# First attention of a four-layer network: values stationary in 32-column tiles, scores in 64-row tile pairs, ScalarE copies ahead of exponentials, outputs turned in their own bank

## The reference, cut to what matters

```python
q = _qdq(x) @ _qdq(wq).T + bq
kv = cond @ wkv.T + bkv
...
attn = jax.nn.softmax(jnp.einsum('bnhd,bmhd->bhnm', q, k) * scale, axis=-1)
o = jnp.einsum('bhnm,bmhd->bnhd', attn, v).reshape(B, N, C)
out = _qdq(o) @ _qdq(wp).T + bp
```

## Time and profile before

| | us |
|---|---|
| three runs | 843.74, 844.09, 846.97 (median 844.09) |
| span of the profiled execution | 847.4 |
| PE busy in the span | 760.9 (90%) |
| DVE busy | 576.4 (68%) |
| ACT busy | 379.8 (45%) |
| POOL busy | 374.7 (44%) |

### The profile page before, as it was taken

How to read it: one execution, slowest core, us unless ns; L and a number is a source line. 1 busy time by engine, 2 the same in 40 slices (tenths; PEclk the granted TensorE clock), 3 DMA queues, 4 the chain that set the end, 5 groups by cost and what they waited for, 6 DMA issues and landing times.

```text
span 847.4 us, 13816 instructions
## 1 busy us (share of the span) xinstructions
PE 760.9 (90%) x4696; PEld 437.9 (52%) x4696; DVE 576.4 (68%) x1247; ACT 379.8 (45%) x652; POOL 374.7 (44%) x397
## 2 busy tenths in 40 slices
PE   7999999999999887777888989889999999999883
PEld 4557776544357322222333635445558967687531
DVE  5988876379664889998999896876521135025854
ACT  3444443311101798887999253655203343421211
POOL 3524304035132277787888542201160047971435
PEclk9999999999999999998999999999999999988998
DMA  9500002002520789999999300620953142991013
GB/s 299 115 1 1 1 1 78 17 0 48 102 50 1 125 160 188 176 185 176 193 186 185 53 1 24 153 89 14 223 147 122 44 143 70 291 218 46 5 15 36
DMA packets 225996, 84.36 MB, mean 100 GB/s; under 512 B 188003, under 2 KB 224000, under 8 KB 225936
## 3 DMA queue, kind: packets, MB, share of 16 engines
q1 hardware_dynamic: 222992, 78.33, 43.1%
q0 software_dynamic: 2944, 5.25, 2.7%
HBM read 33.21 MB, written 8.40 MB: 49 GB/s over the span
## 4 chain that ended last, share of the span: by engine, by line
PE 55%; DVE 13%; DMA 11%; issue 9%; POOL 7%; ACT 3%; SPq 1%; POOLq 0%; DVEq 0%; ACTq 0%
DMA hT<-hT 6%; PE psum L485 5%; POOL hT L1249 5%; PE psum L660 4%; DMA xn<-hT 4%; PE psum L1759 3%; PE psum L640 3%; DVE psum L1314 3%; PE psum L524 3%; PE psum L1430 2%; PE psum L489 2%; DVE cx L2387 2%; PE psum L2037 2%; PE psum L465 2%; PE psum L612 2%
## 5 line engine op out<-in xcount | busy, mean ns | idle before, releaser
L1314 DVE TENSOR_SCALAR_CACHE_REDUCE psum<-psum,arena 128x1024 f32<-128x1024 f32 x128 | 158.0, 1285 | 11.4 <-PE psum L1136 11.0
L336 POOL TENSOR_TENSOR rstd<-ve,neg_half 128x1 f32<-128x1 f32 x64 | 39.2, 616 | 181.2 <-DVE ve L326 180.4
L1136 PE MATMUL psum<-arena 128*128 128x512 bf16 x256 | 79.7, 394 | 36.8 <-ACT arena L1220 24.5
L1249 POOL TENSOR_SCALAR hT<-arena 128x1024 f16<-128x1024 f32 x86 | 89.8, 1045 | 42.5 <-ACT arena L1220 22.4
L1220 ACT ACTIVATE arena<-psum,am 128x1024 f32<-128x1024 f32 x86 | 95.7, 1114 | 14.0 <-POOL hT L1249 8.4
L719 POOL TENSOR_TENSOR arena<-arena,mask 128x1024 f32<-128x1024 f32 x16 | 32.4, 2046 | 47.9 <-PE psum L640 39.9
L1136 PEld LDWEIGHTS psum<-arena 128*128 (+1 forms) x256 | 15.5, 98 | 71.8 <-issue 34.1
L1249 POOL TENSOR_SCALAR hT<-sg 128x1024 f16<-128x1024 f32 x42 | 43.9, 1045 | 11.1 <-ACT sg L1220 4.3
L1220 ACT ACTIVATE sg<-psum,am 128x1024 f32<-128x1024 f32 x42 | 46.8, 1114 | 4.0 <-DVE psum L1314 2.9
L395 ACT ACTIVATE xT<-psum 128x512 f32<-128x512 f32 x28 | 15.2, 597 | 71.5 <-PE psum L363 71.4
L485 PE MATMUL psum<-xT,arena 128*128 128x512 f32 (+1 forms) x96 | 45.3, 593 | 0.0
(11 more groups left out here) (406 smaller groups left out, 1756.6 us busy)
## 6 DMA issues: line engine op xcount, KB each, us to landing
hT<-in_L_ffn_expert_masks SPq DMA_DIRECT2D x32, 256.0 KB, 3.7
arena<-in_L_ffn_w_gate SPq DMA_DIRECT2D x2, 1408.0 KB
arena<-in_L_ffn_w_up SPq DMA_DIRECT2D x2, 1408.0 KB
arena<-in_L_ffn_w_down SPq DMA_DIRECT2D x2, 1408.0 KB
moe_in<-xT SPq DMA_DIRECT2D x2, 1024.0 KB, 7.0
hT<-moe_in SPq DMA_DIRECT2D x4, 512.0 KB, 5.0
moe_out<-arena SPq DMA_DIRECT2D x16, 128.0 KB, 1.7
hT<-hT SPq DMA_TRANSPOSE x83, 3.3
```

Source lines behind the costliest of these rows:

```text
L336: pool.tensor_tensor(rstd[:, t:t + 1], ve[:, t:t + 1], neg_half[:, t:t + 1], ALU.pow).then_inc(sig("ln_rstd"), 1)
L1136: mm = pe.matmul(psum[:, score_banks(c), :][:, g, :], QT[:, bass.ds(row_tile(j, c), 1), pair, :].rearrange("p t q -> p (t q)"), KT[c % 2][ ...
L1249: pool.tensor_scalar(Y1[:, n % Y_SLOTS, :], pe1(n), 255.0, 1024.0, ALU.mult, ALU.add)\
L1314: dve.tensor_scalar(s, s, size1[:, bass.ds(n, 1)], None, ALU.mult, ALU.min, accum_out=am[:, bass.ds(n, 1)])\
```

## The change

Scores: `kBD0` has half the columns, four heads instead of eight; the upper and the lower 64 rows each hold four heads, so that rows 0 to 63 with 512 columns are step n and rows 64 to 127 step n+1. PE issues the two matmuls of a pair together, into two banks, in even steps. Values: stationary is a slice of 32 columns of `vaug` (16 values, the one, and 15 columns of the next head, whose results nobody reads), moving are the 128 columns of `PT0`; four heads write four strips of 32 partitions of one bank. A batch fills all 512 columns of bank 0 or 1. Then ACT copies the bank (`OT0`), PE transposes it back in four transposes into the same bank, and DVE divides 256 columns at once. ACT exponentiates the fourth head straight from PSUM with the negative maximum as bias and the other three from `SH`; the copy of step n-2 now stands ahead. The factor 1/4 goes into the queries (POOL scales their bias). Transposes have a ring of two banks of their own. Apart from that several loads share a semaphore, and near the end of the program ACT loads eight register values one at a time.

```diff
-        LAG_T0, LAG_V0 = 2, 3
+        LAG_T0, LAG_V0, LAG_C0, LAG_O0 = 2, 3, 4, 5
...
+                if n < STEPS0 and n % 2 == 0:
                     b, i = divmod(n, 4)
                     pe.wait_ge(sig("kbd_ready"), 2 * b + i // 2 + 1)
-                    bank = ring_v.claim(pe)
-                    ids["s0", n] = ring_v.fill(pe.matmul(
-                        bank, qT0[:, i // 2, b * S:(b + 1) * S],
-                        kBD0[:, b % 2, i // 2, 4 * (i % 2):4 * (i % 2) + 4, :].rearrange("p h k -> p (h k)"), start=True, stop=True))
+                    if n >= LAG_V0:
+                        pe.wait_ge(sig("p0_ready"), n - LAG_V0 + 1)
+                    banks = ring_v.claim(pe), ring_v.claim(pe, 1)
+                    for k in range(2):
+                        ids["s0", n + k] = ring_v.fill(pe.matmul(
+                            banks[k], qT0[64 * k:64 * k + 64, i // 2, b * S:(b + 1) * S],
+                            kBD0[64 * k:64 * k + 64, b % 2, i // 2, :, :].rearrange("p h k -> p (h k)"), start=True, stop=True))
+                b, i = divmod(n - LAG_O0, 4)
+                if b >= 0 and i == 3:
+                    pe.wait_ge(sig("out0_copied"), b + 1)
+                    for j in range(4):
+                        mm = pe.transpose(out0(b)[:, j * P:(j + 1) * P], OT0[:, b % 2, j * S:(j + 1) * S], identf)
+                    mm.then_inc(sig("out0_turned"), 1)
...
-                        mm = pe.matmul(bank[:, j * HA:(j + 1) * HA], PT0[:, m % 4, j * S:(j + 1) * S], vaug[:, b, 4 * i + j, :],
-                                       start=True, stop=True)
+                        at = (b * H + 4 * i + j) * HA
+                        mm = pe.matmul(out0(b)[WIDE * j:WIDE * (j + 1), i * S:(i + 1) * S], vaug_flat[:, at:at + WIDE],
+                                       PT0[:, m % 4, j * S:(j + 1) * S], start=True, stop=True)
...
+                    if m == STEPS0 - 1:
+                        pe.wait_ge(sig("out0_read"), NB - 1)
+                        half_T_pe(pe, xn, sig("oq_ready"), lambda t: t + 1, 0)
                         keys1_pe(pe, 6, 7)
...
-            half_T_pe(pe, xn, sig("oq_ready"), lambda t: t + 1, 0)
+            pe.wait_ge(sig("out0_read"), NB)
             keys1_pe(pe, 7, NB)
...
+                b, i = divmod(n - LAG_C0, 4)
+                if b >= 0 and i == 3:
+                    act.wait_ge(sig("v0_done"), 4 * b + 4)
+                    if b >= 2:
+                        act.wait_ge(sig("out0_turned"), b - 1)
+                    act.activation(OT0[:, b % 2, :], out0(b), ACT.Copy).then_inc(sig("out0_copied"), 1)
+                m = n - LAG_T0
+                if 0 <= m < STEPS0:
+                    if m >= 4:
+                        act.wait_ge(sig("v0_done"), m - 3)
+                    bank = ring_t.take(act)
+                    ring_t.release(act.activation(PT0[:, m % 4, :], bank, ACT.Copy))
                 if n < STEPS0:
                     act.wait_ge(ring_v.evacuated, ids["s0", n])
                     p = SH[:, n % 4, :, :]
-                    act.activation(p, p, ACT.Exp, scale=HD ** -0.5).then_inc(sig("p0_ready"), 1)
...
+                    act.activation(p[:, 3, :], ring_v.banks[(ids["s0", n] - 1) % 4][:, 3 * S:], ACT.Exp, bias=am[:, 4 * n + 3:4 * n + 4])
+                    act.activation(p[:, 0:3, :], p[:, 0:3, :], ACT.Exp).then_inc(sig("p0_ready"), 1)
...
-                    ring_v.release(dve.tensor_tensor(SH[:, n % 4, :, :], s, bc(mx.unsqueeze(2), [P, 4, S]), ALU.subtract))
+                        dve.wait_ge(ring_t.full, ids["t0", n - 4])
+                    ring_v.release(dve.tensor_tensor(SH[:, n % 4, 0:3, :], s[:, 0:3, :], bc(mx[:, 0:3].unsqueeze(2), [P, 3, S]), ALU.add))
...
-            regs = [act.alloc_register(f"finished{i}") for i in range(NB)]
-            act.load(regs, finished[0:1, :])
             act.wait_ge(sig("meta_loaded"), 16)
             for i in range(NB):
-                act.wait_ge(ring_v.evacuated, act.snap(regs[i], min_val=1, max_val=ring_v.taken + WALK))
+                done = act.value_load(finished[0:1, i:i + 1], min_val=1, max_val=ring_v.taken + WALK)
+                act.wait_ge(ring_v.evacuated, done)
```

More of the change, by code:

```diff
@@ L29 @@
 HA = HD + 1
+WIDE = 32
+PAD_V = WIDE - HA
 HALF = T // 2
@@ L215, in build @@
         qT0, kT0 = a.tile([DC, T]), a.tile([DC, T])
-        kBD0 = a.tile([2, DC, H // DC, S])
+        kBD0 = a.tile([2, DC, 4, S])
+        mask4 = a.tile([4])
+        a.at += 8 * DC * S - 4
         SH = a.tile([4, 4, S])
@@ L221, in build @@
         Bg, Bu, Bd = a.tile([F0]), a.tile([F0]), a.tile([D])
+        a.at = 20976
+        OT0 = a.tile([2, 4 * S])
         a = Arena(arena)
@@ L674, in xa0_act, with heads @@
                 weight_T_act(act, dst)
-            act.wait_ge(sig("b0_loaded"), 32)
-            def heads(dst, bias):
+            act.wait_ge(sig("small0_loaded"), 64)
+            def heads(dst, bias, scale=1.0):
                 for o in range(DC):
@@ L680, in heads @@
                         bank = ring_a.take(act)
-                        ring_a.release(act.activation(dst[:, o, g * HALF:(g + 1) * HALF], bank, ACT.Identity, bias=bias[:, o:o + 1]))
+                        ring_a.release(act.activation(dst[:, o, g * HALF:(g + 1) * HALF], bank, ACT.Identity, bias=bias[:, o:o + 1],
+                                                      scale=scale))
             heads(kT0, bk0)
@@ L699, in xa0_act @@
                     p = SH[:, n % 4, :, :]
-                    act.activation(p, p, ACT.Exp, scale=HD ** -0.5).then_inc(sig("p0_ready"), 1)
[L701 to L706, removed]
+                    act.activation(p[:, 3, :], ring_v.banks[(ids["s0", n] - 1) % 4][:, 3 * S:], ACT.Exp, bias=am[:, 4 * n + 3:4 * n + 4])
+                    act.activation(p[:, 0:3, :], p[:, 0:3, :], ACT.Exp).then_inc(sig("p0_ready"), 1)
+            half_T_act(act, xT, 0)
             keys1_act(act, 6, 7)
-            half_T_act(act, xT, 0)
             keys1_act(act, 7, NB)
@@ L724, in xa0_dve @@
             dve.wait_ge(sig("w0_loaded"), 16 * 2)
-            for w, ready in ((w_q0, "wq_ready"), (w_p0, "wp_ready")):
-                qdq_dve(dve, step, [w[:, o, :] for o in range(DC)], [tmp[:, o, :] for o in range(DC)], sig(ready),
+            for w in (w_q0, w_p0):
+                qdq_dve(dve, step, [w[:, o, :] for o in range(DC)], [tmp[:, o, :] for o in range(DC)], sig("w0_ready"),
                         lambda i: None)
@@ L748, in round_out @@
                    .then_inc(sig("oq_ready"), 1)
-            for n in range(STEPS0 + LAG_V0):
+            for n in range(STEPS0 + LAG_O0):
                 if n < STEPS0:
+                    dve.wait_ge(ring_v.full, ids["s0", n | 1])
                     bank = ring_v.take(dve)
@@ L771, in xa0_dve @@
-                    if i == 3:
-                        dve.wait_ge(ring_v.evacuated, done)
-                        large0 = step(dve.tensor_reduce(q8[:, 0, b:b + 1], xn[:, b, :], AX.X, ALU.max, apply_absolute_value=True))
-                    elif i == 0 and b >= 1:
-                        scale_out(b - 1, large0)
-                    elif i == 1 and b >= 1:
-                        round_out(b - 1)
+                    dve.tensor_tensor(xn[:, b, :].rearrange("p (h d) -> p h d", h=H), o[:, :, 0:HD],
+                                      bc(inv.unsqueeze(2), [P, H, HD]), ALU.mult).then_inc(sig("out0_read"), 1)
@@ L778, in xa0_dve @@
+                    dve.wait_ge(sig("out0_read"), b + 1)
+                    large0 = step(dve.tensor_reduce(q8[:, 0, b:b + 1], xn[:, b, :], AX.X, ALU.max, apply_absolute_value=True))
+                elif b >= 1 and i == 0:
+                    scale_out(b - 1, large0)
+                elif b >= 1 and i == 1:
+                    round_out(b - 1)
             scale_out(NB - 1, large0)
@@ L2260, in ff3_act @@
             act.wait_ge(ring_v.evacuated, ids["logits3"])
[L2261 removed]
+            act.activation(scr3, probs3, ACT.Exp).then_inc(sig("route_exp_ready"), 1)
             for g in range(2):
```

125 lines of the change are left out of this document (64 added, 61 removed).

## The result

The first comparison gave a median of 833.83 us (832.07, 833.64, 834.02, 841.54) against 843.91 for the kernel before (842.74 to 846.97): ratio 0.9879, 95% interval 0.983 to 0.9928. That is inside the range, but 8.5 us above the forecast, and only half of the 18.8 us seemed to have arrived.

| series | before, mean (n) | changed, mean (n) | difference of the means | ratio, 95% interval |
|---|---|---|---|---|
| first | 844.4 (4) | 835.3 (4) | 9.1 | 0.9879 (0.983 to 0.9928) |
| second | 846.8 (25) | 830.6 (6) | 16.2 | 0.9801 (0.9761 to 0.9841) |
| third | 848.8 (11) | 832.5 (6) | 16.4 | 0.9836 (0.9792 to 0.9881) |
| fourth | 850.0 (17) | 830.1 (6) | 19.9 | 0.9737 (0.9668 to 0.9806) |

A forecast was written before the change was run, and what follows sets the result against it. The prediction took PE to bound the first attention (9.45 of 9.50 us busy per batch). 7.50 x (9.55 - 7.0) = 19.1, less 0.3 for the tail, is 18.8 us: 844.1 becomes 825.3, range 820 to 835.

The forecast's parts named there:

- The batch: First attention, one batch of four steps: 9.55 us before, forecast 7.0, with DVE the longest list.
- DVE's list: DVE's operations per batch in the first attention, summed to 6.9 us against PE's 6.4.
- the 0.1 of friction: First attention: 0.1 us per batch added to DVE's 6.9 because the scores' wait just fits, giving 7.0.
- the scores' loop: First attention: from DVE's subtraction to new scores takes 3.3 us, while DVE has 3.4 of other work; just fits.
- the formula: First attention's gain: 7.50 batches times the shortening of a batch, 7.50 x (9.55 - 7.0) = 19.1 us.
- ten changes of form: PE's switches of tile form per batch: two inside the pairs' 1.06, eight at 0.15 us each, 1.2 in all.
- The tail: From DVE's last maximum to the projection: 10.88 us before, 10.9 to 11.3 forecast, 0.3 charged.
- At nothing: Joined semaphores, POOL's key copies and ACT's register loads near the end: claimed to cost no time.
- A: First attention: PE stays the bound by its form changes, or the scores' loop binds; 829 us, chance 0.20.
- B: First attention: tiles run one after another; 834 us, chance 0.09, or 840 or slower, chance 0.03.
- C: First attention: the granted clock falls to 0.50, making the kernel 14 us slower, 858; chance 0.03.
- the stages behind start earlier by the same amount, whatever the base: Stages after the first attention: the 18.8 us saving carries through whole, 847.4 becoming 828.6 and 844.1 becoming 825.3.

The follow-up runs named there:

- the score experiment: Changed kernel, but each score matmul takes all 128 rows, two in sequence instead of a pair of 64 rows: 839.52 us, ratio 0.9926 to the kernel before.
- the first experiment: Kernel before, old first attention, with only the joined semaphores and ACT's eight separate register loads: median 845.58 us, ratio 0.9987.

## Why the prediction was right, and what was off

- **The batch.** Forecast 7.0, measured 6.88 from the fourth batch on. DVE's list was 6.9 in the sum; the 0.1 of friction wasn't there, so the scores' loop (3.3 against 3.4 in the text) does fit. The first two batches are shorter still (6.38 and 5.89), the third 7.08. From DVE's first maximum to its last it is 47.55 to 100.11, 52.56 against 71.67: 19.1 gained, the number of the sum. That it meets it to the tenth is luck. With 6.88 the formula gives 7.50 x (9.55 - 6.88) = 20.0; but it counts every part of the stage like one of the middle, and the first batch gained only 0.9 (7.32 before), the second 3.7, and what follows the start of the last 1.4 (7.07 before, 5.68 now). That the batches of the middle came out shorter than forecast and the ends longer cancels.
- **PE.** Forecast 6.4, measured 6.3: 2 x 1.06, values 4 x 0.36, transposes 0.53, 2 x 0.56 and 0.59, turning 0.49; the score experiment gives 6.22. The sum has a slip here: of ten changes of form four, not two, belong to the two pairs (each has an entry and an exit in its 1.06), so six at 0.15 were left, 6.1 in all. What PE takes above the 5.2 without changes is 1.1, so the 1.2 was right by size and each of the six is dearer than taken. The rows of the changes: transposes in a row start 0.11 apart, 0.44 for four; behind values or pairs a group takes 0.49 to 0.59, so at the transposes a change costs 0.05 to 0.1, and a group of values takes 0.36 where half of the 0.43 of rows 6 is 0.22, 0.14 more. The rule of the Trainium skill (TensorEngine Tiling (Array Packing), Key Properties), that a change of tiling mode drains TensorE, agrees in kind; in the changed kernel that is about 0.2 for each change at most (1.1 over six), and PE, not being the bound, hides it.
- **ACT** has 5.46 per batch where the sum had 5.7: 0.37 for the fourth head (0.42 taken), 0.51 for three (0.54), 0.59 for a copy.
- **The tail** was charged 0.3; measured 10.65 against 10.88 (110.76 - 100.11), 0.2 gained.
- **At nothing**: held, within the 0.2% of the first experiment. The stage started 0.7 earlier in the first execution, but over all profiles with it the start lies between 47.4 and 49.1, against 47.9 to 48.2 with the old one. The difference stands already at the first matmuls of the context's products (10.80 before, 10.05 in the first execution, 11.01 in the second), and from there to the first maximum it is 37.4 to 37.5 in all three.
- **Rivals.** A is out (DVE waits for scores three times among the first steps, 2.5 us in all, and then not again), B by the experiments with one strip and with 128 rows, C because the clock is 1.00 in the batch. By the Trainium skill's rule on transposes (TensorE: Matmul & The Clock Gate, Part 4, PE-mode transpose) C was likely; none of the changed kernel's four profiles has a fall between 48 and 110 us (of the variants one had, at 104, for 3.4 us, in the tail), so what the prediction had drawn from the rule did not happen, as in rows 9 and 10; what the transposes alone count for no run here shows.

**The step that was off** is "the stages behind start earlier by the same amount, whatever the base", with its "847.4 becomes 828.6 and 844.1 becomes 825.3". The gain of stage and tail was right (18.8 forecast, 19.1 + 0.2 measured) and its base was not. I took the median of three executions, 844.1, and read the profiled one as 0.4% long. It was not long: of the 53 later executions 32 have a shorter span than its 847.4 and 21 a longer one, and their mean time is 848.2. 848.2 - 18.8 is 829.4; the changed kernel's mean is 831.8. The rest, and the scatter, is the term that was missing: the granted clock behind the stage, 711.8 to 721.1 us for the same instructions. The forecast named the clock for the first attention only. That the first median, 833.83, stood at rival B's 834 was chance; it stayed inside the range because of the width that had been left for A and B, not because the forecast had allowed for the scatter behind the stage.

**What stays open.** The traces give 19.1 + 0.2 = 19.3 for stage and tail, the executions 17.7 plus or minus 1.2 at equal clock. The 1.6 between them may be the lines' fit, the chips, or a real loss behind (the first experiment alone leaves room for 1.8); profiles whose stretch behind differs by 9 us can't tell.

## What to carry to other kernels

Tiles that run side by side pay in full only until the next engine's list is reached: add up every engine's list of one round, and take the longest. Here a change of tile form cost about 0.1 to 0.2 us, less than what the tiles saved (0.53 per group of values, 0.82 per pair of scores). And a total that scatters by 1% is no measure for a term of 0.5%: read the term off the trace, and take the base from as many executions as the claim needs, with their granted clock beside them.

## What the hardware showed beyond that

An operation of DVE from SBUF to SBUF was held up by one of POOL. In the kernel with the values in one strip DVE's rounding fell beside POOL's key copies. POOL's timeline, then DVE's:

```profile
76.42 2.04 POOL L758 TENSOR_TENSOR arena<-arena 128x512 f32<-128x512 f32 x2 [6.83 <-PE psum L656]
```

```profile
77.62 0.97 DVE L784 TENSOR_SCALAR hT<-xn,q 128x256 f32<-128x256 f32 x1
78.64 0.35 DVE L786 TENSOR_SCALAR xn<-hT,q 128x256 f32<-128x256 f32 x1
```

DVE's first operation ends at 78.59, just behind the end of POOL's at 78.46, and takes 0.97 instead of 0.35; the same happened in each batch with a key copy beside it (0.97 or 0.98 four times, 0.34 in the batch without one), and DVE's operations that read PSUM were not lengthened (a maximum 0.69 and a subtraction 0.56 beside the same POOL operation). The Trainium skill (Perfetto Trace Analysis, Optimizing Scalar/DVE Operations) says that the two engines share a read port of SBUF, which an operation of DVE with two ports holds for itself. The rows agree with a shared port, in the other direction: there DVE is the one that waits. In the changed kernel the rounding at 64.86 takes 0.54 and ends at 65.40, 0.14 behind POOL's end at 65.26; in the three later batches with a key copy it starts only 0.2 ahead of POOL's end and takes its normal 0.35. So where such an operation falls beside one of POOL is a part of its price.
